# A sixth x @ Wu tile beside the layer-1 maxima, the first tile in two halves around the last count transposes

## The reference, cut to what matters

```
L0: xn = layer_norm(x)
    out1 = gat(xn, W1: 768 -> 4 heads x 192)      # "layer 1", heads 0..3
    out2 = gat(out1, W2: 768 -> 2 heads x 96)     # "layer 2", heads 4, 5
    L0   = concat(x, out2) @ Wu + bu              # Wu: (768 + 192) x 768
x = layernorm(x + L0)
x = layernorm(x + gcn2(x))                        # two GCN layers, 768 x 768

gat, one head:
    h = x @ W;  e = leaky_relu(s_src[src] + s_dst[dst])
    ee = exp(e - segment_max(e, dst));  out = sum(ee * h[src]) / sum(ee)
```

## Time and profile before

| | |
|---|---|
| median of 3 runs | 848.27 us (843.99 to 848.43) |
| span of the profiled execution | 844.9 us, 11,861 instructions |
| PE busy | 794.5 us (94%) |
| DVE busy | 589.5 us (70%) |
| ACT busy | 295.4 us (35%) |
| POOL busy | 24.7 us (3%) |
| mean granted TensorE clock | 0.965 of full speed |

### The profile page before, as it was taken

One profiled execution on the slowest core, in us unless ns is written; L12 is line 12 of the kernel. 1 busy time (PEld: TensorE's weight loads), 2 busy tenths in 40 slices (PEclk: granted clock), 3 DMA queues, 4 the chain that ended last, 5 costly groups with the idle time before them and its releaser, 6 DMA issues.

```text
span 844.9 us, 11861 instructions
## 1 busy us (share of the span) xinstructions
PE 794.5 (94%) x4286; PEld 668.6 (79%) x4286; DVE 589.5 (70%) x1211; ACT 295.4 (35%) x577; POOL 24.7 (3%) x35
## 2 busy tenths in 40 slices
PE   5899999998997999999898998899979999999997
PEld 4856666665665999999666896688878889999996
DVE  2798887885999999996997998666625632212444
ACT  4446666665433344432323452122221311111000
POOL 5100000000000400000000000000000000000000
PEclk9999999999988999999898988899999999999998
DMA  9300000000003201100002300000003000000111
GB/s 316 134 2 1 1 2 2 2 1 1 0 1 122 68 1 63 63 1 1 1 1 89 115 1 2 1 1 1 1 2 130 1 1 1 1 1 19 57 56 52
DMA packets 10541, 27.77 MB, mean 33 GB/s; under 512 B 666, under 2 KB 4076, under 8 KB 9969
## 3 DMA queue, kind: packets, MB, share of 16 engines
q1 hardware_dynamic: 10480, 26.97, 9.2%
HBM read 23.09 MB, written 3.88 MB: 32 GB/s over the span
## 4 chain that ended last, share of the span: by engine, by line
PE 80%; DVE 9%; issue 7%; ACT 2%; DMA 1%; SPq 1%; DVEq 0%
PE ps L1090 77%; DVE att L639 2%; DVE att L675 2%; PE ps L1179 1%; DMA edges<-in_dst 1%; DVE out L662 1%; PE ps L1200 1%; PE ps L1233 1%; PE ps L1383 1%; DVE scrap1b L521 0%; DVE h2x L662 0%; DVE stats L726 0%; DVE mx L521 0%; PE ps L1365 0%; DVE scrap L521 0%
## 5 line engine op out<-in xcount | busy, mean ns | idle before, releaser
L1090 PE MATMUL ps<-g,att 128*128 128x193 f32 x800 | 133.6, 331 | 6.1 <-DVE att L639 6.1
L1090 PEld LDWEIGHTS ps<-g,att 128*128 128x128 f32 x800 | 132.9, 193 | 6.9 <-issue 6.7
L956 ACT ACTIVATE att<-att,ssrc 128x1250 f32<-128x1250 f32 x60 | 80.2, 1338 | 93.1 <-DVE att L675 92.9
L639 DVE SCALAR_TENSOR_TENSOR att<-att,ct 128x1250 f32<-128x1250 f32 x60 | 88.0, 1468 | 7.9 <-ACT att L956 7.7
L675 DVE SCALAR_TENSOR_TENSOR att<-uB,s 128x1250 f32<-128x1250 f32 x60 | 91.1, 1523 | 0.0
L1090 PE MATMUL ps<-wp,xT 128*128 128x388 f32 x240 | 87.5, 502 | 0.8 <-ACT xT L900 0.8
L1090 PE MATMUL ps<-yhi,ctr 128*128 128x384 f32 x200 | 67.7, 338 | 0.0
L739 DVE SCALAR_TENSOR_TENSOR ylo_a<-ps,dinv,yhi 128x384 fp32r<-128x384 f32 x32 | 19.0, 616 | 62.0 <-ACT yhi L828 62.0
L1090 PEld LDWEIGHTS ps<-wp,xT 128*128 128x128 f32 x240 | 42.5, 190 | 24.9 <-issue 1.0
L1090 PE MATMUL ps<-h2x,att 128*128 128x97 f32 x400 | 51.0, 293 | 4.2 <-DVE att L639 2.8
L828 ACT ACTIVATE yhi<-ps,dinv 128x384 fp32r<-128x384 f32 x40 | 22.2, 581 | 93.1 <-PE ps L1090 93.1
(11 more groups left out here) (243 smaller groups left out, 1441.5 us busy)
## 6 DMA issues: line engine op xcount, KB each, us to landing
uB<-u_dram SPq DMA_DIRECT2D x4, 1280.0 KB, 5.9
wux<-in_L_gnn_Wu SPq DMA_DIRECT2D x2, 2304.0 KB, 15.8
gw<-in_L_gnn_W SPq DMA_DIRECT2D x2, 2304.0 KB, 11.1
xs<-in_x SPq DMA_DIRECT2D x1, 3456.0 KB
out<-ybuf SPq DMA_DIRECT2D x9, 384.0 KB, 2.3
w<-in_L_gnn_W SPq DMA_DIRECT2D x2, 1152.0 KB, 7.0
w2x<-in_L_gnn_W SPq DMA_DIRECT2D x1, 576.0 KB, 7.5
wuo<-in_L_gnn_Wu SPq DMA_DIRECT2D x1, 576.0 KB
```

The lines of the kernel that those rows point to most:

```text
L639: v.scalar_tensor_tensor(a, a, HUGE, ct[:, q, 0:N], ALU.min, ALU.mult).then_inc(att_ready, 1)
L956: a.activation(at_, at_, ACT.Exp, bias=ssrc[:, h, q:q + 1]).then_inc(att_exp, 1)
L1090: return t.matmul(o, lhsT, rhs, start=start, stop=stop, **kw)
```

## The change

X2 goes from 5 to 6: tile 5 of x @ Wu moves from stage B to stage A. In stage A, the order of PE and ACT changes as well. The transposes of tile 0 and the first half of its product now come ahead of `count_transposes(T - 1, 1)`, and the second half behind it. For q = 1 to 3 the transposes of tile q come ahead of the source rows of head q, and the product of the same tile q follows them; before, it was the product of tile q - 1. In stage B, the rows of head 4 are broadcast at q == T - 1 instead of q == T - 2: behind the product of tile 8 instead of tile 7. With tile 5 gone from the stage, two products stand between the two broadcasts as before, and none behind the second.

```diff
-X2 = 5
+X2 = 6
@@ block.scalar (ACT)
             for n in range(3):
                 source_piece(n)
+            x_transposed(0)
             counts_out(T - 1)
-            x_transposed(0)
+            x_out2(0)
             counts_done(T - 1, 1)
             for q in range(1, H1):
+                x_transposed(q)
                 for n in range(3 * q, 3 * q + 3):
                     source_piece(n)
-                if q < H1 - 1:
-                    x_transposed(q)
-                    x_out2(q - 1)
+                x_out2(q)
+            x_transposed(H1)
             broadcast_u(0)
             a.wait_ge(deg_ready, 1)
             a.activation(sqd[:, :], deg[:, :], ACT.Sqrt).then_inc(sq_ready, 1)
-            for q in range(H1 - 1, X2 + 1):
-                if q < X2:
-                    x_transposed(q)
-                x_out2(q - 1)
+            for q in range(H1, X2):
+                if q + 1 < X2:
+                    x_transposed(q + 1)
+                x_out2(q)
...
-                elif q == T - 2:
+                elif q == T - 1:
                     broadcast_u(H1)
@@ block.tensor (PE)
             t.wait_ge(bc_out, 3)
-            count_transposes(T - 1, 1)
             t.wait_ge(dn_out, 2 * T + 2)
             x_transposes(0)
+            t.wait_ge(wu_plus, KD)
+            x_wu_half(0, 0, 0)
+            count_transposes(T - 1, 1)
+            x_wu_half(0, 1, 1)
             t.wait_ge(cp_deg, 3 * T + 4)
-            t.wait_ge(wu_plus, KD)
             for q in range(1, H1):
+                x_transposes(q)
                 source_rows(3 * q, 3 * q + 3)
-                if q < H1 - 1:
-                    x_transposes(q)
-                    x_wu(q - 1)
+                x_wu(q)
+            x_transposes(H1)
             t.wait_ge(bc_out, SRC1)
             broadcast_u(0)
             t.wait_ge(dmax_ready, 1)
             t.transpose(ps[0:1, 5, 0:P], degmax[:, :], identf[:, :]).then_inc(dmax_ps, 1)
-            for q in range(H1 - 1, X2 + 1):
-                if q < X2:
-                    x_transposes(q)
-                x_wu(q - 1)
+            for q in range(H1, X2):
+                if q + 1 < X2:
+                    x_transposes(q + 1)
+                x_wu(q)
...
-                elif q == T - 2:
+                elif q == T - 1:
                     broadcast_u(H1)
```

## The result

The changed kernel takes 852.32 us (median of 5 runs, 851.63 to 853.46). The kernel before takes 847.97 us (median of now 5 runs, 843.99 to 848.43). The ratio is 1.0063, with a 95% interval of 1.0039 to 1.0087. It is slower by about 4.4 us, where +1.2 was forecast: the time lies inside the range of the prediction, but it is a loss that can be told from no change, and I had given that a chance of 0.10.

The account below looks back on a forecast made before the run. PE, busy 94% of the span, was taken to end stage B and be level with DVE in stage A. +6.9 (stage A) - 6.2 (stage B) + 0.5 (head 4) = +1.2 on 848.27, so 849.5 us, range 844.8 to 852.8.

Parts of the forecast that it names:

- Stage B's end is PE's, DVE is 6 us behind: End of stage B before the change: PE sets it, and DVE stands idle 6.09 us for head 4's first exponent.
- Stage B gives 6.2 us back: Stage B: without the moved tile DVE's first row releases head 4, so its exponent starts 6.2 us earlier.
- Stage A costs 6.9 us: Stage A: PE's longer list delays ACT's last copy, so head 0's exponent starts 6.9 us later.
- the wait: Stage A, ahead of tile 1's product: PE idles 0.7 us for ACT's copies of tile 1's transposes.
- The bound I gave for one stretch more: Stage A, around the broadcast for head 0: one more stretch at the lower clock would add 3.4 us.
- The table load is hidden: Before head 0's exponent: the 1.28 us load runs beside DVE's memset and row, 1.3 against 1.6 us, costing 0.
- The start of head 4, +0.5: Head 4's first tiles: after a longer PE idle gap they run longer at the lower clock, costing 0.5 us.
- Layer-1 heads, 0: The layer-1 heads after stage A: PE bounds them and their length stays unchanged, so nothing is counted.
- Rival 1: Stage A: the denser list keeps PE's clock up, costing 2.5 instead of 6.9 us; 845.1 us in all, chance 0.14.
- Rival 2: Stage A: the new wait before tile 1's product brings a lower-clock stretch of 3.4 us; 852.9 us, chance 0.14.
- Rival 3: Stage B: a lower-clock stretch is missing in most executions, so the gain is only 3.8 us; 851.9 us, chance 0.12.
- My sign of being wrong: Forecast wrong if stage A's end moves under 4 or over 9 us, or head 4's exponent trails DVE's row over 2.

Follow-up runs that it names:

- a1: The kernel before, with the window ranges that VectorE and TensorE load in the counts stage clamped from below; 848.22 us, ratio 1.0018 to the kernel before.
- a2: The changed kernel with the same clamp of the window ranges as a1; 851.91 us, ratio 1.0070 to the kernel before.
- b1: a2 with 20 of the 24 instructions of tile 5's product left out in stage A, so another result is computed; 844.23 us, ratio 0.9967.
- b2: a2 with layer 2's source rows broadcast between the halves of tile 6's product in stage B instead of behind both; 851.62 us, ratio 1.0054.
- c2: a2 run once more, unchanged, for one trace; 849.90 us (one run).

## Why the prediction was wrong

The forecast was +1.2 us and the spans differ by 5.0. Of the 3.8 us between, 1.75 are stage B, which gave less, and 1.7 stage A, which cost more; 1.8 lie ahead of stage A, which the sum didn't hold and which come and go from trace to trace; the rest of the kernel was 1.45 us better than forecast. In the pair a1 and a2, stage B's 1.7 us is the larger miss, and stage A's is 0.3.

- **Stage B's end is PE's, DVE is 6 us behind: right.** After the change the chain goes through DVE's maxima, and DVE no longer waits for the first exponent.
- **Stage B gives 6.2 us back: the step that failed.** Measured 4.45 (4.46 in a2 against a1), alike in all three traces of the changed kernel. I took DVE's own start as fixed ("which PE's lists feed exactly as before"). It hangs on PE's first product of the stage, and part of that ran at the lower clock in the new timing: the first maximum came at 19.0 instead of 17.3. From there to the exponent DVE takes 31.0 us in a2, b1 and b2 alike, so the 1.7 us pass on in full. The list was the same, the clock was not. b2 shows the dependence by removing it. Why the clock was down at that place stays open.
- **Stage A costs 6.9 us: mechanism right, too small.** Measured 7.2 (a2), 8.4 (c2) and 8.6. The terms for the tile, the rows and the wait were right: one period of rows, transposes and tile is 9.5 us in the new list too, and the wait is 0.78. What was mis-sized is the clock at the start. I charged 0.45 us for 0.9 us of lower clock; in two of three traces the stretch was 6.8 us long and the first half product took 6.3 and 6.2 us instead of 3.9, in the third 3.4 long and the half 5.8. In the trace after, PE reached the product of tile 1 2.2 us later behind the start of the stage than forecast. The broadcast, where I had left the 6.8 us stretch, had 3.4. The bound I gave for one stretch more (+3.4) holds this in size, but I had put it at the broadcast.
- **The table load is hidden: right**, 1.6 us from copy to exponent (1.7 forecast). The Trainium skill ("ScalarE: Activation LUTs", What ACT_TABLE_LOAD costs) gives about 2.66 us for the whole switch; the trace is against it here as well, with 1.6 us from the load's start to the exponent's.
- **The start of head 4, +0.5: right.** From exponent to collect 35.8 (after) and 35.7 (a2), against 35.3. What the Trainium skill ("TensorE: Matmul & The Clock Gate", What's actually happening) says of the throttled state as the default agrees with the trace there: 13.7 us at 0.50 over the gap.
- **Layer-1 heads, 0: they gave 0.75 back**, with PE 3.3 instead of 4.4 us at the lower clock at head 0's start. By half of the 1.1 us that is 0.55 of it, an estimate.
- **The rivals.** Rival 1 (clock stays up in stage A) fell. Rival 2 named the wrong place: the clock did cost stage A more, but ahead of the count transposes, not behind the new wait, where it stayed up. Its 852.9 us and rival 3's 851.9 are near the measured 852.3 by luck. Rival 3 had the right sign, stage B giving less, by the wrong reason: the old end was 54.44 to 54.45 in all three traces of the old kernel. Those are three executions; the runs differ by more than that (843.99 to 848.43), and how often a stretch is missing in the others isn't shown.
- **My sign of being wrong**, stage A's end moving by more than 9 us: from the start of the span it moved by 10.4, from the start of the stage by 8.6.

With the measured terms, 7.2 to 8.6 less 4.45, less 0.8, plus 0.4, the sum is +2.4 to +3.8. a2's median is 3.7 above a1's, its trace 2.5.

## What to carry to other kernels

Moving work gains only what the emptied stage's next engine allows, and it costs in full where the receiving stage has no idle time: where the engines are level at the end of a stage, the added instructions are paid one for one. Look for the gap that the same engine already has in the schedule (here 1.4 us between two heads), and for the wait that holds the next engine's start. Where the next engine hangs on one long piece of work, that piece can be split around the hand-off: in b2 the first maximum came at 16.82 us though the half ahead of it ran at the lower clock. That pays only where this engine ends the stage, and only if what follows doesn't lose it again, as b2's head 4 did. Read from the chain which engine ends the stage before crediting a gain to an edit.

## What I had not expected of the hardware

In stage B, the stretches at the lower clock fell in the same places relative to the work, within a microsecond, in all kept traces of one kernel (three of the old: the first product of stage B at the full clock and 54.44 to 54.45 us; three of the changed: partly at the lower one and 49.98 to 50.00), and they moved when work far ahead of them changed length. In b1, 20 instructions fewer in stage A went with a stage B 1.65 us shorter, 150 us later. In stage A the places were less fixed (6.8 us in two traces of the changed kernel, 3.4 in the third). Here, then, a term of a sum that holds such a stretch depends on the timing of the whole kernel, and not only on the stage that it stands in.
